# Node stages of a four-layer graph network: from loops over pairs of node tiles to pipelines written out over whole tensors

## The reference, cut to what matters

```python
h = jnp.maximum(_layernorm(x, axis=-1), 0.0)
x = x + _L0_gnn_ref(h, ...)      # typed attention over edges; ends in a matmul with one of 4 matrices, by node type
h = jnp.maximum(_layernorm(x, axis=-1), 0.0)
x = x + _L1_gnn_ref(h, ...)      # h @ weight, then a softmax over 4 heads for the first 3125 edges only
h = jnp.maximum(_layernorm(x, axis=-1), 0.0)
x = x + _L2_gnn_ref(h, ...)      # sum of neighbours, routed experts, normalisation over all nodes
h = jnp.maximum(_layernorm(x, axis=-1), 0.0)
x = x + _L3_gnn_ref(h, ...)      # Q, K, V from h + 0.1 * query; attention over edges; @ Wo; layernorm
```

## Time and profile before

| | |
|---|---|
| runs | 6745.78, 6691.39, 6702.11 us; median 6702.11 |
| profiled execution | 6654.7 us, span 6653.1 us |
| busy in the span | PE 64%, DVE 54%, POOL 47%, ACT 33% |
| mean granted TensorE clock | 0.795 |
| l1n and l2n | 1979.9 to 2490.1 us |
| l3n | 4596.8 to 4921.4 us |
| fin | 6446.5 to 6653.1 us |

### The profile page before, as it was taken

How to read it: one execution, slowest core, us unless ns; L and a number is a source line. 1 busy time by engine, 2 the same in 40 slices (tenths; PEclk the granted TensorE clock), 3 DMA queues, 4 the chain that set the end, 5 groups by cost and what they waited for, 6 DMA issues and landing times. The chain is left out here.

```text
span 6653.1 us, 94389 instructions
## 1 busy us (share of the span) xinstructions
PE 4281.8 (64%) x25484; PEld 3173.8 (48%) x25484; DVE 3563.9 (54%) x7285; ACT 2224.7 (33%) x7694; POOL 3118.9 (47%) x3164
## 2 busy tenths in 40 slices
PE   3898577777767305655555558884657677776754
PEld 2665455656545204443443447772225555555542
DVE  3454688888863442222221311114249999998875
ACT  1332466666652210000000112221115555555540
POOL 0340677777750127777777020002036666666620
PEclk8999788888889656677776879995668888888875
DMA  5333788888871224333334067832147777777752
GB/s 184 119 131 116 224 260 260 253 255 260 254 173 57 59 76 123 103 103 104 104 104 97 9 213 261 262 113 84 63 149 221 222 228 223 229 226 220 224 130 73
DMA packets 559988, 1092.90 MB, mean 164 GB/s; under 512 B 129764, under 2 KB 372456, under 8 KB 556061
## 3 DMA queue, kind: packets, MB, share of 16 engines
q0 software_dynamic: 204144, 617.42, 32.2%
q1 hardware_dynamic: 355434, 470.78, 21.7%
HBM read 973.54 MB, written 201.47 MB: 177 GB/s over the span
## 5 line engine op out<-in xcount | busy, mean ns | idle before, releaser
L738 POOL DMA_INDIRECT l3e_kv<-t_table,k_recs x912 | 986.9, 1082 | 489.0 <-issue 250.7
L1394 PE MATMUL l2e_pA<-l2e_row,l2e_oh 128*128 128x257 f32 x1824 | 691.1, 545 | 742.7 <-issue 474.3
L738 POOL DMA_INDIRECT l0e_kv<-t_table,k_recs x912 | 966.9, 1060 | 292.3 <-issue 258.1
L1348 POOL DMA_INDIRECT l2e_row<-t_table,l2e_idx x912 | 882.3, 967 | 278.5 <-issue 277.5
L1394 PEld LDWEIGHTS l2e_pA<-l2e_row,l2e_oh 128*128 128x128 f32 x1824 | 472.2, 271 | 961.3 <-issue 870.4
L1015 ACT ACTIVATE l0e_vw<-l0e_kv,l0e_w 128x64 f32<-128x64 f32 x2736 | 679.8, 334 | 0.1
L1015 ACT ACTIVATE l3e_vw<-l3e_kv,l3e_w 128x64 f32<-128x64 f32 x2736 | 679.8, 334 | 0.0
L924 PE MATMUL l3e_pQE<-l3e_qb,l3e_ohT 128*128 128x256 bf16 x2736 | 412.1, 311 | 389.7 <-issue 359.4
L1373 DVE SCALAR_TENSOR_TENSOR l2e_acc<-l2e_acc,k_itf,l2e_pA 128x257 f32<-128x257 f32 x228 | 109.9, 482 | 929.4 <-issue 872.6
L972 PE MATMUL l0e_pA<-l0e_vw,l0e_ohf 128*128 128x260 f32 x1824 | 545.4, 451 | 11.0 <-ACT l0e_vw L1015 7.8
L924 PEld LDWEIGHTS l3e_pQE<-l3e_qb,l3e_ohT 128*128 128x128 bf16 x2736 | 290.9, 109 | 485.7 <-issue 410.7
(11 more groups left out here) (456 smaller groups left out, 7447.4 us busy)
## 6 DMA issues: line engine op xcount, KB each, us to landing
exp_w<-in_L_gnn_w SPq DMA_DIRECT2D x224, 512.0 KB
t_table<-l0n_tab SPq DMA_DIRECT2D x26, 2048.0 KB, 6.9
l0e_qb<-t_q SPq DMA_DIRECT2D x228, 192.0 KB, 6.0
l3e_qb<-t_q SPq DMA_DIRECT2D x228, 192.0 KB, 4.1
t_agg<-l0e_acc SPq DMA_DIRECT2D x228, 130.0 KB
t_agg<-l3e_acc SPq DMA_DIRECT2D x228, 130.0 KB
l0e_drow<-t_drow SPq DMA_DIRECT2D x57, 512.0 KB, 6.5
l3e_drow<-t_drow SPq DMA_DIRECT2D x57, 512.0 KB, 6.3
```

The lines of the kernel that those rows point to most:

```text
L738: pool.indirect_dma_start(kv[:, n % SK, g, :], None, table[:, :], bass.IndirectOffsetOnAxis(ap=K["recs"][:, n, g, ridx:ridx + 1], axis=0)) ...
L1348: pool.indirect_dma_start(row[:, s, g, 0:D], None, table[:, :], bass.IndirectOffsetOnAxis(ap=idx[:, i, g:g + 1], axis=0)).then_inc(row_rea ...
L1394: last = pe.matmul(pA[s % 2][:, 0:W], oh[:, s, g, :], row[:, s, g, :], start=(g == 0), stop=(g == G - 1))
```

## The change

l1n and l2n become one stage, l12n. x (`moe_xx`), the normalised rows and h2 stay on chip for all 26 tiles, so x1 and h2 are no longer stored and loaded again; the type masks and the degree factors stay in K from l0n on, so `rdego` is not stored at the end of l0n, and `tmask` is not loaded again by l1n, l2e and comb. All steps are written out per tile or per chunk of tiles, without loops. Loads come in chunks (`AT`, `CT`). The type selection moves behind the matmul: PE multiplies the scaled rows with all four matrices (four matmuls of 512 columns), and DVE adds the four results with the mask as scalar. The indices of all 52 gathers are loaded at the start of l12n by ACT's queue, in runs of four bytes. The gathers start when the whole table is stored. comb loads layer 3's weights and leaves x3 on chip; its store moves into l3n, ahead of everything else on SP's queue. In l3n the bias is split by POOL into three bf16 rows and added by a bf16 matmul of three rows. In fin the masking of V and the adding of beta move from DVE to POOL.

```diff
@@ layer0_nodes
-            with nc.allow_non_contiguous_dma(reason="3328 degrees, once"):
-                sp.dma_start(T["rdego"].rearrange("(b p) c -> p (b c)", p=P), dego[:, :]).then_inc(stored, 16)
...
+def layer12_nodes(nc, A, T, K, M):
+        TB = 4
+        AT = (0, 2, 8, 14, 20, NBP)
+        GT = (0, 4, 8, 12, 16, 20, 24, NBP)
...
+        @block.sync
+            for j, (a, b) in enumerate(zip(AT, AT[1:])):
+                sp.dma_start(big[:, a:b, 0:H * HV], chunk("agg0", a, b)).then_inc(ag_in[j], 16)
+                if j == 0:
+                    for c in range(2):
+                        sp.dma_start(wa[:, c, :, :], A["L0_gnn_a_linears"][:, c * P:(c + 1) * P, :].rearrange("t p n -> p t n")).then_inc(wa_in, 16)
+                sp.dma_start(x[:, a:b, :], chunk("x0", a, b)).then_inc(x_in[j], 16)
+            for t in range(NBP):
+                sp.wait_ge(tb_ready, t + 1)
+                sp.dma_start(rows(T["table1"], t * P), tb[:, t % TB, :]).then_inc(tb_out[t % TB], 16)
...
+        @block.gpsimd
+            pool.wait_ge(edges_in, 32)
+            for u in range(TB):
+                pool.wait_ge(tb_out[u], 32 * ((NBP - 1 - u) // TB + 1))
+            for t in range(NBP):
+                j = t // GW
+                pool.indirect_dma_start(gd[:, t, :], None, T["table1"][:, :], bass.IndirectOffsetOnAxis(ap=di[:, t:t + 1], axis=0)).then_inc(g_in[j], 16)
+                pool.indirect_dma_start(gs[:, t, :], None, T["tablel"][:, :], bass.IndirectOffsetOnAxis(ap=si[:, t:t + 1], axis=0)).then_inc(g_in[j], 16)
...
+        @block.vector
+            def typed(t):
+                dve.wait_ge(o_ps, t + 1)
+                for k in range(NT):
+                    last = dve.scalar_tensor_tensor(out=x[:, t, :], in0=pO[t % 2][:, k, :], scalar=K["mask"][:, t, 1, k:k + 1], in1=x[:, t, :],
+                                                    op0=ALU.mult, op1=ALU.add)
+                    if k < NT - 1:
+                        dve.drain()
+                last.then_inc(x1_ready, 1)
+                dve.drain()
+                dve.bn_stats(st[:, t, :], x[:, t, :])
...
+            for t in range(NBP + 2):
+                for j in range(1, NA):
+                    if t == max(AT[j] - 4, 1):
+                        scale(j)
+                if 0 <= t - 1 < NBP:
+                    typed(t - 1)
+                if 0 <= t - 2 < NBP:
+                    normal(t - 2)
...
+            for j in range(NG + 1):
+                if j < NG:
+                    scores(j)
+                if j:
+                    normal2(j - 1)
+                if j < NG:
+                    heads_mean(j)
...
+        @block.tensor
+            def outputs(t):
+                pe.wait_ge(aT_ready, t + 1)
+                if t >= 2:
+                    pe.wait_ge(x1_ready, t - 1)
+                for o in range(2):
+                    for c in range(2):
+                        last = pe.matmul(pO[t % 2][:, 2 * o:2 * o + 2, :].rearrange("p k n -> p (k n)"), aT[:, t % 2, c, :],
+                                         wa[:, c, 2 * o:2 * o + 2, :].rearrange("p k n -> p (k n)"), start=(c == 0), stop=(c == 1))
...
+        @block.scalar
+            act.dma_start(wx[:, :, 0:D], A["L1_gnn_weight"].rearrange("(c p) n -> p c n", p=P)).then_inc(wx_in, 16)
...
+                for t, a in ((si, "src"), (di, "dst")):
+                    act.dma_start(t[:, :], A[a][0:NP].rearrange("(b p) -> p b", p=P)).then_inc(edges_in, 16)
...
@@ combine
-            sp.dma_start(mk[:, :, :], T["tmask"].rearrange("(b p) c -> p b c", p=P)).then_inc(c_in, 16)
...
-            for j in range(4):
-                sp.wait_ge(out_ready, j + 1)
-                sp.dma_start(T["x3"].rearrange("(b p) c -> p b c", p=P)[:, Q0[j]:Q0[j] + QB[j], :], quarter(X2, j)).then_inc(stored, 16)
-            sp.wait_ge(stored, 64)
+            for j, a in enumerate("qkv"):
+                sp.dma_start(M["w3"][:, :, j, :], A[f"L3_gnn_W{a}"].rearrange("(c p) n -> p c n", p=P)).then_inc(next_in, 16)
...
@@ layer3_nodes
+        CT = (0, 2, 8, 14, 20, NBP)
...
+            sp.dma_start(chunk("x3", 0, NBP), x[:, :, :]).then_inc(x_out, 16)
...
+        @block.gpsimd
+            pool.tensor_copy(bp[:, 0, :], bias)
+            pool.drain()
+            pool.tensor_tensor(br[:, :], bias, bp[:, 0, :], ALU.subtract)
...
+            pool.drain().then_inc(bias_ready, 1)
...
+        @block.tensor
+            def projected(t):
+                pe.wait_ge(eT_ready, t + 1)
+                if t >= 2:
+                    pe.wait_ge(kv_ready, t - 1)
+                    pe.wait_ge(q_split, t - 1)
...
+                    for c in range(2):
+                        pe.matmul(out, eT[:, t % 2, c, :], rhs(c), start=(c == 0), stop=False)
+                    last = pe.matmul(out, oneb[:, :], bias, start=False, stop=True)
...
+            for t in range(NBP + 1):
+                if t < NBP:
+                    turned(t)
+                if t == 1:
+                    pe.wait_ge(bias_ready, 1)
+                if t:
+                    projected(t - 1)
...
@@ output
+        CT = (0, 2, 7, 12, 17, 21, NB)
...
+            for j, (c0, c1) in enumerate(zip(CT, CT[1:])):
+                sp.dma_start(ag[:, c0:c1, :, :].rearrange("p b h c -> p b (h c)"), chunk(T["agg3"], c0, c1)).then_inc(ag_in[j], 16)
...
+        @block.gpsimd
+            for j, (c0, c1) in enumerate(zip(CT, CT[1:])):
+                pool.wait_ge(v_in[j], 16)
+                pool.wait_ge(none_ready, j + 1)
+                pool.tensor_tensor(heads(v[:, c0:c1, :]), heads(v[:, c0:c1, :]), none[:, c0:c1, :].unsqueeze(3).to_broadcast([P, c1 - c0, H, DK]), ALU.mult).then_inc(v_masked, 1)
+                pool.wait_ge(x_in[j], 16)
+                pool.tensor_tensor(x[:, c0:c1, :], x[:, c0:c1, :], gb[:, 1, :].unsqueeze(1).to_broadcast([P, c1 - c0, D]), ALU.add).then_inc(x_shifted, 1)
...
+            emptied(0)
+            emptied(1)
+            mixed(0)
+            dve.wait_ge(gb_in, 32)
+            for j in range(NC + 1):
+                if j + 2 < NC:
+                    emptied(j + 2)
+                if j + 1 < NC:
+                    mixed(j + 1)
+                if j < NC:
+                    residual(j)
+                if j:
+                    scaled(j - 1)
```

More of the change, by code:

```diff
@@ new lines, in turned_h @@
+            def turned_h(t):
+                pe.wait_ge(h_ready, t + 1)
+                if t:
+                    pe.wait_ge(hT_ready, t)
+                for c in range(2):
+                    last = pe.transpose(pH[:, c, :], h[:, t, c * P:(c + 1) * P], K["ident"][:, :])
+                last.then_inc(h_ps, 1)
+            def projected(t):
+                pe.wait_ge(hT_ready, t + 1)
+                if t >= 2:
+                    pe.wait_ge(tb_ready, t - 1)
+                for c in range(2):
+                    last = pe.matmul(pX[t % 2][:, 0:WX], hT[:, t % 2, c, :], wx[:, c, :], start=(c == 0), stop=(c == 1))
+                last.then_inc(x_ps, 1)
@@ L2218, in _, with turned, projected @@
-            over_blocks(pe, step)
+            def turned(t):
+                for j in range(NC):
+                    if t == CT[j]:
+                        pe.wait_ge(a_ready, j + 1)
+                if t >= 2:
+                    pe.wait_ge(aT_ready, t - 1)
+                for c in range(2):
+                    last = pe.transpose(pA[t % 2][:, c, :], a[:, t, c * P:(c + 1) * P], K["ident"][:, :])
+                last.then_inc(a_ps, 1)
+            def projected(t):
+                pe.wait_ge(aT_ready, t + 1)
+                if t >= 4:
+                    pe.wait_ge(o_used, t - 3)
+                for c in range(2):
+                    pe.matmul(pO[t % 4][:, 0:D], aT[:, t % 2, c, :], w[:, c, :], start=(c == 0), stop=False)
+                pe.matmul(pO[t % 4][:, 0:D], K["ones"][0:1, :], bo[:, :], start=False, stop=True).then_inc(o_ps, 1)
@@ L2220, in _ @@
+            turned(0)
+            pe.wait_ge(w_in, 32)
+            for t in range(NB):
+                if t + 1 < NB and t + 1 not in CT:
+                    turned(t + 1)
+                projected(t)
+                if t + 1 < NB and t + 1 in CT:
+                    turned(t + 1)
         @block.scalar
         def _(act):
[L2222 to L2228 removed]
```

859 lines of the change are left out of this document (429 added, 430 removed).

## The result

The changed kernel takes 6120.1 us (median of four runs, 6106.0 to 6171.7), the kernel before 6699.3 (four runs). The medians lie 579 us apart; the ratio is 0.915 with a 95% interval of 0.911 to 0.920, so 8.5% faster. The forecast was 6134, within 6050 to 6250.

A forecast was written before the change was run, and what follows sets the result against it. Node stages were held bound by chains of waits between engines. Gains of 14 (l0n), 246 (l12n), 8 (comb), 206 (l3n) and 94 (fin), 568 us, gave 6087 profiled, 6134 us as run median; range 6050 to 6250.

The forecast's parts named there:

- The mechanism: Node stages l1n, l2n, l3n, fin: they pay for chains; once tiles overlap, the engine with most work sets the pace.
- tiles do not overlap: Rival, l12n, l3n, fin: some wait holds PE until its own tile is through; 293 us more, 6427 us; chance 4%.
- clock stays low: Rival, l12n and l3n: PE stays at half clock; 208 us more, 6342 us; chance 7%.
- DVE does not starve the gathers: Denies a rival for l12n: busy DVE slows the gathers, 7 us or up to 22, 6156 us; chance 7%.
- No item stage slowed down: Denies a rival: gathers of the item stages grow by 0.25 us with moved tables, 6818 us; chance 2%.
- 26 x 5.3 and 5 cold: l12n, first half: PE sets 5.3 us a tile, 138 us for 26 tiles, plus 5 for a cold clock.
- The gathers' part: l12n, second half: 12 us for first gathers, 69 at DVE's 2.65 a tile, 8 at the end; 89 us.
- DVE's sum for the first half: l12n, first half: DVE needs 4.1 us a tile, upper bound 4.7, below PE's 5.3.
- the prediction's 3.5: l3n: PE at full clock bounds at 3.5 us a tile (3.2 to 4.6), 91 us for 26 tiles.
- 25 x 3.0: fin: DVE sets the pace at 3.0 us a tile, 75 us for 25 tiles.
- The 12 us for POOL's passes: fin: what moving two passes to POOL costs DVE; 12 us taken, between nothing and 28.
- The sign that fin is at 3.3 us a tile with DVE as its busiest engine: fin: expected in the changed profile if the prediction held, a tile every 3.3 us and DVE busiest.

The follow-up runs named there:

- serial_order: Changed kernel with every engine doing all steps of a tile before the next in l12n's first half and l3n: l12n 463.6 us, l3n 289.8 us.

## Why the prediction came out right, and where it did not

**The mechanism** was right where a run tests it: without the overlap of tiles the first half of l12n loses 218 us, more than the 106 it had gained, and l3n 163 of its 197. For the gather half and fin it is argued from the waits. The rival "tiles do not overlap" was priced too low, 218 us for these two stages where `serial_order` lost 381: it had PE's waits right (128 and 84 us, 140 and 78 priced) and left out the busy time that grows as the clock falls with them. The rival "clock stays low" did not come in l12n and l3n. DVE does not starve the gathers (1.25 us apart). No item stage slowed down beyond its scatter (l0e 4.5 us longer, 1312 to 1320 us in the kernels of this chip that leave it alone).

**l12n, 22 us better than predicted.** By the bounds of the earlier trace rows (from DVE's last instruction in l0e at 2003.8) it is 241.5 us, predicted 264. The term "26 x 5.3 and 5 cold" was mis-sized: 121.9 us from the start of the first product to the end of the last and not 143. I had added busy times of groups (3.72 + 0.52 + 1.16), but the modelled ends of a group lie over the next group's start: in the new trace, too, the four groups' busy times add up to (95.2 + 28.8 + 10.5 + 10.4) / 26 = 5.57 us a tile, and the products are 4.76 apart. The start was 17.9 us and not 23; the end to the first gather 12.8 and not 8.5. The gathers' part met its 89 us (88.8), though POOL set its pace and not DVE: the 52 gathers start over 68.7 us, and DVE works 57.9, 2.2 us a tile and not 2.65. DVE's sum for the first half was also added up wrongly: its terms give 3.7 us a tile, or 4.3 with nothing taken off, and not 4.1 and 4.7; measured are 90.4 us, 3.5 a tile, and nothing hung on it.

**l3n, 9 us worse.** First product at 15.9 us, with POOL's bias as the last thing waited for (13 taken, 3 to 15 the bound for POOL's steps). The pace was 3.68 us a tile with 0.62 for the bias rows, where 0.3 were taken for a range of nothing to 1.4; the parts of the prediction's 3.5 add up to 3.4. Two tiles came later still, 5.6 and 5.3 us, with PE waiting for DVE, whose statistics of the next six tiles stand ahead of its step. No term held this.

```profile
4386.78 0.56 PE L2140 MATMUL l3n_pE<-k_ident,l3n_en 128*128 128x128 f32 x2 [1.78 <-DVE l3n_en L2105]
```

From the start of the first product to the end of the last tile it is 103.8 us, 95 with the cold start predicted; the end 7.1 for 11.

**fin, 22 us worse, and the step that failed.** I took DVE's busy time for the pace ("25 x 3.0") and PE only as the cause of a short ring wait of two matmuls at 1.91 us. PE's whole tile at half clock is 0.48 + 1.85 + 1.15 = 3.48 us, more than DVE's 3.0; the bias row and the turn were not counted at all. That the clock would stay at 0.50 was used for one wait and not for the sum. Start 15.9 (20 predicted), PE 101.9 (67 + 6 + 12), end 17.4 (8): DVE still has two chunks to scale behind PE's last product. The 12 us for POOL's passes were no price at all here, though one of the prediction's signs of being wrong, passes above 3 us, did come (3.69). The sign that fin is at 3.3 us a tile with DVE as its busiest engine failed: it is 20.26 / 5 = 4.05, and PE is busy 89.8 us, DVE 79.8. The rule cited there (the Trainium skill, SBUF — State Buffer, "Who interferes with whom"), by which a DVE instruction with both inputs on chip is locked out while GpSimd reads, is what the rows show (1.49 us became 3.46); the 129 us worked out from it come near the measured 135 for another reason, PE's.

**l0n, 33 us off.** The term was right (12.6 for 14). But the stage before it ran differently: its reciprocal stands at 687.4 us and not 654.9. These are stretches in l0n, one of the kernel before and two of the kernel after, in this order:

```profile
540.00:580.00 40.00, 36.48 (x218) 25.72 (x217) 19.56 (x35) 12.72 (x22) 0.00 (x0) 1.00 0.31 121
```

```profile
540.00:580.00 40.00, 37.67 (x208) 26.96 (x207) 20.25 (x34) 9.72 (x17) 0.00 (x0) 0.83 0.30 117
580.00:620.00 40.00, 39.80 (x193) 26.34 (x193) 17.37 (x26) 8.56 (x16) 0.00 (x0) 0.74 0.31 121
```

The code is the same and PE no less busy, and the granted clock is 1.00 in one and 0.83 and 0.74 in the other. Over the twelve traces without the store, l0n is 643.2 us + 0.348 for each us at half clock (90 us there: 672.5; 261 us: 734.6; correlation 0.998). The trace of before, with 72 us, has the least of all. By the slope the clock would make 25 of the 32.5 us; 7 stay open. It would also explain part of why the profiled execution of before lay 44.6 us under its median; that is argued, as the other runs have no trace. The forecast carried that offset of 47 us over whole, which was 52 us too much, since the new profiled execution lies 5 over its median; the sum against the traces was 38 too large. The two cancel to the 14 us by which 6134 missed, and so do 22 us too little in l12n and 22 too much in fin: that it came so near is luck. The lower end of the range has no full account: its terms add up to 6071, not 6050. The measured median lies inside either way.

**comb, 5 us too high a gain.** x2's load was issued 2.3 us earlier in the stage, but landed only 1.1 earlier, 20.3 us after its start, and the gathers took 1.2 us more; the end gave 4.3 where 3 was taken.

```profile
4238.94 0.48 DVE L1942 SCALAR_TENSOR_TENSOR comb_Y<-comb_ya,k_share,comb_tmp 128x256 f32<-128x256 f32 x1 [6.82 <-DMA moe_x<-t_x]
```

The 8.5 us less in l0e, l2e, gate, exp and l3e together are within what these stages differ by between kernels that leave them alone (l2e 1176 to 1186, exp 583 to 593 on this chip).

## What to carry to other kernels

To find a pipeline's pace, write down for every engine the whole list of one tile, PE's turns and bias rows too, at the clock that it will have, from start to start and not as a sum of busy times; the largest sets it. An idle stretch behind a load is only worth what stands next behind it: a load moved to another queue still sends its traffic, so move it in time. Before moving a pass to another engine ask how long a single pass may block its neighbour, and how far ahead of the bound that neighbour runs.
